# Layer 1 of a two-layer cross-attention: VectorE's mask adds of key pairs 2 and 4 become identity matmuls in PSUM

## The reference, cut to what matters

```python
scores = jnp.einsum('bkgld,bksd->bkgls', q, k) * scale
scores = scores + encoder_attention_mask[:, :, None, :, :]
attn = jax.nn.softmax(scores, axis=-1)
out = jnp.einsum('bkgls,bksd->bkgld', attn, v)
```

## Time and profile before

| | us |
|---|---|
| median of 3 runs | 4795.5 |
| lowest and highest | 4792.86, 4804.38 |
| profiled execution, its time | 4799.57 |
| profiled execution, its span (first to last instruction) | 4797.8 |
| busy in the span: PE, DVE, ACT, POOL | 4070.1, 3115.7, 2364.9, 2191.9 |
| mean granted clock of TensorE | 0.943 of full speed |

### The profile page before, as it was taken

How to read it: one execution, slowest core, us unless ns; L and a number is a source line. 1 busy time by engine, 2 the same in 40 slices (tenths; PEclk the granted TensorE clock), 3 DMA queues, 4 the chain that set the end, 5 groups by cost and what they waited for, 6 DMA issues and landing times. The chain is left out here.

```text
span 4797.8 us, 54201 instructions
## 1 busy us (share of the span) xinstructions
PE 4070.1 (85%) x17152; PEld 2035.2 (42%) x17152; DVE 3115.7 (65%) x7393; ACT 2364.9 (49%) x2796; POOL 2191.9 (46%) x1036
## 2 busy tenths in 40 slices
PE   8888988886888898888688889888868888988886
PEld 4333654442444355444244336544424343654442
DVE  3556568885356656888535565688853556568885
ACT  1444237775144423777514442377751444237775
POOL 1655026664155602666416550266641655026664
PEclk9999999998989999999999999999989999999998
DMA  3112321110311232111031123211103112321110
GB/s 104 36 36 58 110 68 25 25 25 14 103 36 36 58 110 68 25 25 25 14 103 36 36 58 110 68 25 25 25 14 103 36 36 58 110 68 25 25 25 14
DMA packets 115778, 240.59 MB, mean 50 GB/s; under 512 B 26244, under 2 KB 47492, under 8 KB 106760
## 3 DMA queue, kind: packets, MB, share of 16 engines
q1 hardware_dynamic: 111048, 231.52, 19.3%
q10 hardware_dynamic: 4416, 5.30, 0.5%
HBM read 117.15 MB, written 4.19 MB: 25 GB/s over the span
## 5 line engine op out<-in xcount | busy, mean ns | idle before, releaser
L915 POOL TENSOR_TENSOR l_pt<-l_pt,l_maskT 128x1024 f32<-128x1024 f32 x512 | 1215.1, 2384 | 753.4 <-ACT l_pt L933 753.4
L963 DVE CUSTOM_DVE_ANT_0 tile_b<-l_psR,hT 128x400 f32<-128x400 f32 (+1 forms) x2048 | 1076.5, 570 | 251.0 <-PE l_psR L1042 250.7
L378 DVE TENSOR_REDUCE l_acc<-l_psR 128x1 f32<-128x424 f32 (+1 forms) x1280 | 698.4, 589 | 482.9 <-PE l_psR L467 471.8
L943 ACT ACTIVATE l_pt<-l_pt 128x1024 f32<-128x1024 f32 (+1 forms) x896 | 874.1, 991 | 19.9 <-POOL l_pt L915 2.3
L1075 PE MATMUL l_psO<-l_pt,V 128*32 128x512 f32 (+1 forms) x3328 | 557.4, 623 | 261.3 <-ACT l_pt L943 261.3
L1042 PE MATMUL l_psR<-split_w,qst 128*128 128x400 f32 (+1 forms) x2048 | 710.0, 406 | 59.4 <-DVE tile_b L997 27.0
L300 POOL TENSOR_TENSOR l_psum<-l_psum,l_pt 128x1024 f32<-128x1024 f32 x280 | 664.9, 2375 | 154.9 <-ACT l_pt L350 135.0
L350 ACT ACTIVATE l_pt<-l_psB 128x1024 f32<-128x1024 f32 (+1 forms) x576 | 550.8, 977 | 370.1 <-PE l_psB L489 354.0
L933 ACT ACTIVATE l_pt<-l_psB 128x1024 f32<-128x1024 f32 x512 | 524.1, 1024 | 305.8 <-PE l_psB L1064 304.9
L467 PE MATMUL l_psR<-l_kst,l_qst 128*128 128x424 f32 (+1 forms) x1280 | 491.6, 425 | 166.3 <-DVE l_acc L378 94.1
L1042 PEld LDWEIGHTS l_psR<-split_w,qst 128*128 128x128 f32 x2048 | 381.6, 196 | 550.5 <-DVE l_acc L963 343.2
(11 more groups left out here) (119 smaller groups left out, 4088.9 us busy)
## 6 DMA issues: line engine op xcount, KB each, us to landing
l_kst<-l_khl SPq DMA_DIRECT2D x192, 264.1 KB, 3.8
mid_w<-in_w SPq DMA_DIRECT2D x128, 256.0 KB, 4.1
qst<-q SPq DMA_DIRECT2D x512, 32.0 KB, 2.0
qst<-qlast SPq DMA_DIRECT2D x128, 128.0 KB, 2.4
hT<-in_maskN SPq DMA_DIRECT2D x16, 800.5 KB, 10.7
split_w<-k SPq DMA_DIRECT2D x128, 100.1 KB, 3.6
l_qst<-l_qhl SPq DMA_DIRECT2D x192, 64.0 KB, 2.0
l_maskT<-in_maskT SPq DMA_DIRECT2D x48, 256.0 KB
```

The lines of the kernel that those rows point to most:

```text
L378: dve.tensor_reduce(acc[:, h % 2, qt, c:c + 1], psR[:, ring[item] % NR, 0:w], AX.X, ALU.max).then_inc(s_red, 1)
L915: pool.tensor_tensor(tile, tile, maskT[:, kt:kt + 2, :].rearrange("p a n -> p (a n)"), ALU.add)\
L943: act.activation(pt[0:r, n % NPT1, 0:w], pt[0:r, n % NPT1, 0:w], ACT.Exp).then_inc(s_exp, 1)
L963: dve.tensor_tensor_reduce(junk[:, n % 2, 0:hi - lo], psR[:, ring[item] % NR, 0:hi - lo], maskN[:, qt, lo:hi], 1.0, -3e38, ALU.add, ALU.ma ...
```

## The change

Pairs 2 and 4 leave VectorE. TensorE adds their mask in PSUM: after the 2 score matmuls of such a pair come 4 more of 512 columns (two parts of the mask for each of two key tiles), whose weights are the identity and whose moving operand is the mask, split into a high part in fp32r and the remainder. ScalarE then takes the exponential straight from PSUM into `pt`, in the step of the pair itself, behind the P of two steps back; the later exponential in place falls away. The masks of the 4 tiles are loaded first, into `pt`, and GpSimd splits them with 8 instructions of 128 x 512 at the start of the stage, before its own adds. The first copy to `pt`, the first VectorE add and the first B2 wait for that. To make room, parts of `osb` move into free pieces of `hT` and `tile_b`. New waits use semaphores of their own (`s_pexp`, `s_msplit`, `s_raw`).

```diff
+PE_PAIRS = (2, 4)
+PE_KT = [kt for p in PE_PAIRS for kt in (2 * p, 2 * p + 1)]
+OTHER_KT = [kt for kt in range(T1) if kt not in PE_KT]
+LOWEST = -3e38
...
-    maskT = sb("maskT", [P, T1, L])
+    maskT = sb("maskT", [P, len(OTHER_KT), L])
+    maskP = sb("maskP", [P, 2, len(PE_KT), L], F32R)
...
-    osb = sb("osb", [P, 8, L])
+    osb = [keep["hT"][:, q, N1:N1 + L] for q in range(QT)] + [keep["tile_b"][:, 3, :]]
+    osb_own = sb("osb", [P, 8 - len(osb), L])
+    osb += [osb_own[:, i, :] for i in range(8 - len(osb))]
...
+    raw = pt.rearrange("p a (c n) -> p (a c) n", c=2)
...
-        for t in range(T1):
+        for i, t in enumerate(PE_KT):
+            sp.dma_start(raw[:, i, :], ios["maskT"][b, t * P:t * P + P, :]).then_inc(s_raw, 16)
+        for i, t in enumerate(OTHER_KT):
...
-        pool.wait_ge(s_mt, 16 * T1)
+        pool.wait_ge(s_raw, 16 * len(PE_KT))
+        for i in range(len(PE_KT)):
+            pool.tensor_scalar(maskP[:, 0, i, :], raw[:, i, :], LOWEST, None, ALU.max).then_inc(s_msplit, 1)
+        for i in range(len(PE_KT)):
+            pool.wait_ge(s_msplit, i + 1)
+            pool.tensor_tensor(maskP[:, 1, i, :], raw[:, i, :], maskP[:, 0, i, :].bitcast(F32), ALU.subtract)\
+                .then_inc(s_msplit, 1)
+        pool.wait_ge(s_mt, 16 * len(OTHER_KT))
...
+                elif n == 1:
+                    act.wait_ge(s_msplit, 2 * len(PE_KT))
...
-                act.activation(pt[0:r, n % NPT1, 0:w], pt[0:r, n % NPT1, 0:w], ACT.Exp).then_inc(s_exp, 1)
+                if at not in by_pe:
+                    act.activation(pt[0:r, n % NPT1, 0:w], pt[0:r, n % NPT1, 0:w], ACT.Exp).then_inc(s_exp, 1)
+                following = ("B", *divmod(n + 1, PAIRS1))
+                if following in by_pe:
+                    n += 2
+                    act.wait_ge(s_b, n)
+                    if n > NPT1:
+                        act.wait_ge(s_pv, n - NPT1)
+                    act.activation(pt[:, n % NPT1, :], psB[:, 2 * (n % 2):2 * (n % 2) + 2, :].rearrange("p a n -> p (a n)"),
+                                   ACT.Exp).then_inc(s_pexp, 1)
...
+                    elif before in by_pe:
+                        pe.wait_ge(s_pexp, by_pe[before])
...
+                if item in by_pe and by_pe[item] == 1:
+                    pe.wait_ge(s_msplit, 2 * len(PE_KT))
...
-                                   start=True, stop=True)
+                                   start=True, stop=item not in by_pe)
+                for part in range(2 * (item in by_pe)):
+                    for kt in (2 * p, 2 * p + 1):
+                        mm = pe.matmul(psB[:, 2 * (n % 2) + kt % 2, :], ident[:, :], maskP[:, part, PE_KT.index(kt), :],
+                                       start=False, stop=part == 1)
```

More of the change, by code:

```diff
@@ L872, in layer1_attention @@
     s_b, s_add, s_exp, s_pv = sem("l1_b_full"), sem("l1_masked"), sem("l1_exp"), sem("l1_pv")
+    s_raw, s_msplit, s_pexp = sem("l1_maskP_in"), sem("l1_mask_split"), sem("l1_exp_of_psum")
     s_copy, s_padd, s_zero = sem("l1_copied"), sem("l1_masked_by_pool"), sem("l1_zeros")
@@ L884, in layer1_attention @@
     by_pool = order([x for x in plan if x[0] == "B" and x[2] in POOL_PAIRS], "B")
-    by_dve = order([x for x in plan if x[0] == "B" and x[2] not in POOL_PAIRS], "B")
+    by_pe = order([x for x in plan if x[0] == "B" and x[2] in PE_PAIRS], "B")
+    by_dve = order([x for x in plan if x[0] == "B" and x[2] not in POOL_PAIRS + PE_PAIRS], "B")
+    not_pe = order([x for x in plan if x[0] == "B" and x not in by_pe], "B")
+    raw = pt.rearrange("p a (c n) -> p (a c) n", c=2)
     block = ctx.enter_context(nc.Block())
@@ L909, in _ @@
         pool.memset(mz[:, :, :, 0:96].bitcast(F32), 0.0).then_inc(s_zero, 1)
-        pool.wait_ge(s_mt, 16 * T1)
+        pool.wait_ge(s_raw, 16 * len(PE_KT))
[6 more added lines that the diff above has]
+        pool.wait_ge(s_mt, 16 * len(OTHER_KT))
         for item in by_pool:
-            n, kt = bb[item], 2 * item[2]
+            n, kt = bb[item], OTHER_KT.index(2 * item[2])
             pool.wait_ge(s_copy, by_pool[item])
@@ L940, in _ @@
                     act.wait_ge(s_padd, by_pool[at])
[L941 removed]
+                elif at in by_dve:
                     act.wait_ge(s_add, by_dve[at])
[L943 removed]
+                if at not in by_pe:
[8 more added lines that the diff above has]
+                                   ACT.Exp).then_inc(s_pexp, 1)
             elif item[0] == "E":
@@ L948, in _ @@
                     act.wait_ge(s_m, m_uses[("X", h // 8 - 1)])
-                act.activation(osb[:, h % 8, :], psO[:, :], ACT.Copy).then_inc(s_osb, 1)
+                act.activation(osb[h % 8], psO[:, :], ACT.Copy).then_inc(s_osb, 1)
     @block.vector
@@ L983, in _ @@
                 if by_dve[item] == 1:
-                    dve.wait_ge(s_mt, 16 * T1)
+                    dve.wait_ge(s_mt, 16 * len(OTHER_KT))
+                    dve.wait_ge(s_msplit, 2 * len(PE_KT))
                 dve.wait_ge(s_b, n)
@@ L989, in _ @@
                                   psB[0:r, 2 * (n % 2):2 * (n % 2) + 2, :].rearrange("p a n -> p (a n)")[:, 0:w],
-                                  maskT[0:r, kt:kt + w // 512, :].rearrange("p a n -> p (a n)"),
+                                  maskT[0:r, OTHER_KT.index(kt):OTHER_KT.index(kt) + w // 512, :].rearrange("p a n -> p (a n)"),
                                   ALU.add).then_inc(s_add, 1)
@@ L1060, in _ @@
                     before = ("B", *divmod(n - 3, PAIRS1))
-                    pe.wait_ge(s_copy if before in by_pool else s_add, (by_pool if before in by_pool else by_dve)[before])
+                    if before in by_pool:
+                        pe.wait_ge(s_copy, by_pool[before])
+                    elif before in by_pe:
+                        pe.wait_ge(s_pexp, by_pe[before])
+                    else:
+                        pe.wait_ge(s_add, by_dve[before])
+                if item in by_pe and by_pe[item] == 1:
+                    pe.wait_ge(s_msplit, 2 * len(PE_KT))
                 for kt in range(2 * p, min(2 * p + 2, T1)):
@@ L1069, in _ @@
                 n, kv = bb[("B", h, p)], h // GQ
-                pe.wait_ge(s_exp, n + (p % 2 == 0 and p + 1 < PAIRS1))
+                for one in (("B", h, p), ("B", h, p + 1)) if p % 2 == 0 and p + 1 < PAIRS1 else (("B", h, p),):
+                    if one in by_pe:
+                        pe.wait_ge(s_pexp, by_pe[one])
+                    else:
+                        pe.wait_ge(s_exp, not_pe[one])
                 if p == 0 and h:
@@ L1084, in _ @@
                 pe.wait_ge(s_add, len(by_dve))
+                pe.wait_ge(s_pexp, len(by_pe))
                 for q in range(QT):
@@ L1092, in _ @@
                     mm = pe.matmul(psM[32 * (j // 2):32 * (j // 2) + 32, :], sel[:, 1 + 2 * (k == "Y") + j % 2, :],
-                                   osb[:, j, :], start=(j % 2 == 0), stop=(j % 2 == 1), skip_group_check=True)
+                                   osb[j], start=(j % 2 == 0), stop=(j % 2 == 1), skip_group_check=True)
                 mm.then_inc(s_m, 1)
```

2 lines of the change are left out of this document (1 added, 1 removed).

## The result

The changed kernel takes 4995.9 us (median of 4 runs, 4995.8 to 4998.52), the kernel before 4794.18 us (4 runs, 4792.78 to 4804.38). The ratio is 1.0419 with a 95% interval of 1.0406 to 1.0432: 4.2% slower, where 4977 us or 3.8% had been forecast. The profiled execution has a span of 4994.0 us at a mean granted clock of 0.946.

A forecast was written before the change was run, and what follows sets the result against it. No engine full; bound by a chain, TensorE's unbroken first half, then two ScalarE waits. Thirty heads at 1.86 - 0.44 = 1.42 us, plus 2.1 and 0.6, give 45.3 us a batch, 181 us in all: 4977 us, range 4,900 to 5,045.

The forecast's parts named there:

- The two waits: TensorE's waits for ScalarE before W of pairs 2,3 and 4,5: 1.29 and 0.76 us, counted from B5, staying.
- The price of eight additions: Identity matmuls behind B2 and B4, 0.232 us each, 1.86 us a head; bounds 1.7 and 2.5 us.
- 131 ns: Skill page's matmul gap for 512 columns: eight would cost 1.05 us, time about 4,880 us; held contradicted by the middle's row.
- The relief of the ring: Three-bank ring holding up A and M: without pair 2's add M starts earlier, saving 0.44 us; bounds nothing and 0.75.
- the first half of the chain: From W of pairs 4 and 5 to B5's end: TensorE works without a pause, but for a VectorE stretch in step 3.
- ScalarE costs nothing: Exp 2 and exp 4 from PSUM: same instruction count, some 1050 us per 1000, no cost; uncovered, up to 1 us each.
- a sign of being wrong: Wrong if, among others, a wait for the new exponentials (before B4 or B6) or for the split appears.
- The start of the stage: Masks there by about 669, split 10.1 us, 3.8 us left before first copy; VectorE's CAST delay 0.6 us a batch.
- The last two heads: Heads without A matmuls at a batch's end: additions cost 0.9 and 1.2 us, the last at slow clock.
- The sum: Thirty heads at 1.42 us plus 2.1 and 0.6: 45.3 us a batch, four times 181 us; 4977 us.

The follow-up runs named there:

- Experiment 8: Kernel before, with TensorE masking pair 5 alone instead of ScalarE's copy and GpSimd's add, pairs 2 and 4 still on VectorE: 4642.88 us, ratio 0.9679.
- experiment 3: Changed kernel without the eight mask matmuls of a head, so pairs 2 and 4 get no mask: 4799.96 us, ratio 1.0.
- experiment 10: Kernel with TensorE masking pair 5 alone, its four mask matmuls left out so pair 5 has no mask: 4544.21 us, ratio 0.9482 to the kernel before.
- Experiment 6: Changed kernel plus an unused VectorE reduction of 1024 mask elements where the add of pair 2 stood: 5021.49 us, ratio 1.0467 to the kernel before.
- experiment 4: Changed kernel with only pair 2 masked on TensorE, pair 4 staying with VectorE: 4907.67 us, ratio 1.0222 to the kernel before.
- experiment 1: Changed kernel with W of an even pair waiting for one semaphore only, the later pair's exponential: 4948.7 us, ratio 1.0314 to the kernel before.

## Why the prediction was right, point by point

**The two waits lie behind what was added.** Right, and the step on which the sign hung. Both waits stayed (1.37 and 0.85 us) although B2 and B4 grew by 0.93 us each. Experiment 8 shows the other side: with a copy and an add taken out of the path that the waits are for, both waits go, and that is more than the additions behind B5 cost.

**The price of eight additions.** 1.86 us forecast, 1.86 measured, from a row of the same shape elsewhere in the kernel. The 131 ns of the Trainium skill, TensorE: Matmul & The Clock Gate, "Back-to-back issue gap", would have been 1.05 us; the trace doesn't agree and has 0.232 us each. In experiment 3, where they are away, the head is 15.80 - 14.32 = 1.48 us shorter. That is not 1.86, because the relief of the ring, some 0.4 us, finds no use there. In experiment 10 no such second path is in the way, and four matmuls give back 13.06 - 12.12 = 0.94 us, the whole of their 0.93.

**The relief of the ring.** 0.44 us forecast, 0.43 measured, M 1.62 us behind the pair of A (1.61 forecast). Experiment 6 shows the mechanism, with 0.27 us of it. But the reason why it counts was incomplete: the text took the first half of the chain for TensorE's alone. In the kernel before, ScalarE's copy 3 and exp 1 are just as long there (2.74 against 2.75 us), and the relief counts only since pair 4's additions stand in TensorE's path. The expectations of experiments 3 and 4 have the same mistake and were off by it, 13.94 for 14.32 and 14.78 for 15.25. Right in the sum, then, for a reason of which half was missing.

**ScalarE costs nothing.** Right: 1024 ns from PSUM against 1025 of the row read the earlier trace rows; E starts 0.11 us behind the second A pair, as before, and no wait for the new exponentials before B4 or B6 shows.

**The wait in front of W.** Missed. The change splits one wait into two and puts the one that blocks last. At 0.09 us a time, twice a head, it makes 15.80 out of the 15.63 that the other terms give. With the shorter group heads of experiment 1 it was worth some 38 us in this stage (47 between the medians of the two kernels), nearly as much as the ring's 0.43 us a head bring (0.43 x 28 x 4 = 48). The prediction names new waits as a sign of being wrong, and priced only those for the new exponentials and the split.

**The start of the stage.** The split came later than forecast (start 672.7 instead of 669, of which 2.2 us are the later start of the stage itself; 10.8 us instead of 10.1), so of 3.8 us to spare about 2 were left, and the first copy didn't wait. The CAST beside it took 0.29 us and not 0.92, and the subtraction behind that 0.16 us: neither was held until the end of the split's instruction beside it. The prediction had 0.6 us a batch for this, and 2.5 at most. Of the 1.8 us by which the first E comes later, 0.1 lies ahead of the first copy. The rest lies between the first copy and the first E, with twelve additions (B2 and B4 of the first head, B2 of the second) and two reliefs of the ring; it wasn't taken apart further.

**The last two heads.** Forecast at 2.1 us; over the last three intervals of a batch the kernel after is 0.45 us faster (15.31, 14.24 and 20.05 us against 13.68, 15.1 and 21.27). The timeline of the kernel after in the last but one:

```profile
1194.23 1.06 PE L1122 MATMUL l_psO<-l_pt,V 128*32 128x512 f32 x8 [1.68 <-ACT l_pt L966]
1195.23 0.77 PE L1103 MATMUL l_psB<-qst,split_w 128*128 128x512 f32 x2
```

The forecast priced B matmuls at the slow clock, 1.22 us for two. Here two take 0.77, and the W ahead of them 1.06. The clock stayed up, and that pays for the additions. Windows of this interval, before and after:

```profile
1132.64:1147.74 15.10, 10.85 (x44) 3.79 (x44) 3.39 (x4) 11.58 (x13) 10.45 (x5) 0.77 0.01 1
```

```profile
1183.70:1197.94 14.24, 10.40 (x52) 4.63 (x52) 0.69 (x1) 11.58 (x14) 9.45 (x4) 1.00 0.00 0
```

Why it stayed up was not tested, so that these intervals came out cheap is luck for the sum.

**The sum.** Forecast 45.3 us a batch, measured 46.8. The 28 plain and group intervals cost 45.5 us and not 28 x 1.42 = 39.8, most of it for the waits in front of W (28 x 0.17 = 4.8). The last three intervals were forecast at 1.42 + 2.1 = 3.5 us and brought 0.45, and the start was forecast at 1.42 + 0.6 = 2.0 and cost 1.8. So the missed 5.7 us were mostly hidden by 4.0 on the other side: that the forecast is within 19 us of the measured time is in part luck. Of the 196 us between the spans 187 are in the stage; 9 lie in stages that the change doesn't touch.

## What to carry to other kernels

Before work is moved onto an engine, find where that engine waits, and whether the wait is counted from before or from behind the new work; four additions take TensorE 0.93 us in each of the places tried, but instead of an add of VectorE they made the head 1.1 us longer, and instead of the copy and the add that TensorE waited for 1.1 us shorter. A relief counts only if no other path of the same length runs beside it, so look for the second longest path over the same stretch as well. Where an instruction of TensorE needs two semaphores, wait first for the one that will be late.

## What the runs showed of the hardware

- A matmul behind two semaphore waits, of which the second is the one that blocks, starts 0.14 us behind the instruction that it waited for; behind one wait 0.05 us. The blocking one put first gives the same 0.05 us and the same head as one wait. W of pairs 0 and 1, where a third wait (for the E before) stands behind the blocking one, starts 0.10 us behind (experiments 3 and 4).
- Short VectorE instructions of 128 x 4 elements depend on GpSimd: the CAST took 0.18 us with GpSimd idle (experiment 8), 0.92 beside one add and 1.51 beside three in a row, and the subtraction behind it 0.16 with GpSimd idle and 1.91. The long ones end within 0.04 us of the end of the GpSimd add that they started beside. Beside a TENSOR_SCALAR of the split, 1.48 us long, the hold is shorter: a subtraction that starts in its first 0.4 us ends 0.63 us behind its start (1925.55 and 1926.17 in the second batch of the kernel after), one that starts 1.04 us behind its start takes 0.16 us (first batch).
- The 26 matmuls of a group change take 3.0 us at a granted clock of 1.00 and 4.7 at 0.64. The wait of 2.26 us for the reciprocal stands in front of them in both kernels. What decides was not tested; behind equal heads of 15.25 us (experiment 4) both come.
